# A Householder step rearranged: pairs side by side, one correction product, the p column on ScalarE, A x of block 2 on TensorE, fewer zero matmuls

## What is computed

```python
deg = jnp.sum(A, axis=0) + jnp.sum(A, axis=1) - jnp.diagonal(A)
L_norm = d_inv_sqrt[:, None] * (jnp.diag(deg) - A) * d_inv_sqrt[None, :]
_, U = jnp.linalg.eigh(L_norm)
agg = jnp.einsum('mn,bnd->bmd', U.T, features)
h = jax.nn.relu(agg @ W1 + b1)
return jnp.einsum('nm,bmd->bnd', U, h @ W2 + b2)
```

## Time and profile before

| | |
|---|---|
| three runs | 4189.59, 4192.28 and 4192.59 us, median 4192.28 us |
| span of the profiled execution | 4189.8 us |
| busy: TensorE, its loads, VectorE, ScalarE | 81%, 49%, 79%, 37% |
| x of step 2 to last x (L486) | 58.2 to 2189.7 us |

### The profile page before, as it was taken

How to read it: one execution, slowest core, us unless ns; L and a number is a source line. 1 busy time by engine, 2 the same in 40 slices (tenths; PEclk the granted TensorE clock), 3 DMA queues, 4 the chain that set the end, 5 groups by cost and what they waited for, 6 DMA issues and landing times. The chain is left out here.

```text
span 4189.8 us, 62612 instructions
## 1 busy us (share of the span) xinstructions
PE 3382.9 (81%) x14639; PEld 2049.1 (49%) x14827; DVE 3298.6 (79%) x21659; ACT 1532.1 (37%) x5534; POOL 55.6 (1%) x71
## 2 busy tenths in 40 slices
PE   5999999999999999988886576554207999998859
PEld 3555555555555665577774322243103444454337
DVE  7888898889988788999988899999984323454467
ACT  2444444333333333333332322211212324554545
POOL 0000000000000000000000000000000000020000
PEclk9999999999999899955559887755558999999969
DMA  0000000000000000000000000000002000000001
GB/s 11 1 1 1 1 1 1 1 1 1 1 1 1 1 2 2 1 1 1 1 1 1 1 1 1 1 1 1 0 20 50 0 0 0 1 0 0 0 6 36
DMA packets 14163, 16.47 MB, mean 4 GB/s; under 512 B 571, under 2 KB 10214, under 8 KB 13798
## 3 DMA queue, kind: packets, MB, share of 16 engines
q1 hardware_dynamic: 13798, 12.48, 1.1%
HBM read 8.28 MB, written 4.19 MB: 3 GB/s over the span
## 5 line engine op out<-in xcount | busy, mean ns | idle before, releaser
L206 PE MATMUL ps<-zero_stream 128*128 128x512 bf16 x2875 | 845.9, 397 | 9.0 <-issue 2.8
L206 PEld LDWEIGHTS ps<-zero_stream 128*128 128x128 bf16 x3045 | 333.6, 126 | 227.7 <-issue 101.7
L304 ACT ACTIVATE refl<-ps,tiny 128x1 f32<-128x1 f32 x511 | 133.5, 261 | 451.4 <-PE ps L244 287.9
L318 ACT ACTIVATE vectors<-WihT,refl 128x4 f32<-128x4 f32 (+2 forms) x383 | 115.0, 300 | 391.9 <-DVE refl L439 387.3
L255 PEld LDWEIGHTS ps<-dot_parts,ones 128*128 128x128 f32 x766 | 133.2, 201 | 203.6 <-DVE dot_parts L433 179.9
L233 PE MATMUL ps<-ident,vectors 128*128 128x128 f32 x1148 | 214.9, 298 | 14.3 <-DVE vectors L486 1.3
L380 DVE CUSTOM_DVE_ANT_0 products<-ps,UT 128x511 f32<-128x511 f32 (+60 forms) x426 | 215.0, 533 | 13.1 <-PE ps L233 12.5
L486 DVE SCALAR_TENSOR_TENSOR vectors<-x_scaled,ps,y_scaled 128x4 f32<-128x4 f32 (+3 forms) x510 | 116.2, 228 | 134.5 <-PE ps L255 89.9
L233 PEld LDWEIGHTS ps<-ident,vectors 128*128 128x128 f32 x1148 | 124.0, 141 | 191.6 <-DVE vectors L486 186.0
L380 DVE CUSTOM_DVE_ANT_0 products<-ps,U 128x499 f32<-128x499 f32 (+57 forms) x402 | 199.2, 524 | 5.1 <-PE ps L233 4.6
L686 ACT ACTIVATE sturm_signs<-sturm_products,sign_bias 128x576 bf16<-128x576 f32 x96 | 74.4, 775 | 350.8 <-DVE products_mark L713 350.8
(11 more groups left out here) (611 smaller groups left out, 8440.9 us busy)
## 6 DMA issues: line engine op xcount, KB each, us to landing
out_dram<-x SPq DMA_DIRECT2D x16, 256.0 KB, 2.3
adj<-in_adj_dram SPq DMA_DIRECT2D x1, 1024.0 KB, 5.2
l2w_in<-in_L_gnn_W_dram SPq DMA_DIRECT2D x2, 128.0 KB
Wqkv<-in_L_gnn_Wqkv_dram SPq DMA_DIRECT2D x1, 192.0 KB
L_gnn_W<-in_L_gnn_W_dram SPq DMA_DIRECT2D x2, 64.0 KB
L_gnn_Wg<-in_L_gnn_Wg_dram SPq DMA_DIRECT2D x2, 64.0 KB
x<-in_x_dram SPq DMA_DIRECT2D x4, 0.5 KB
L_gnn_Wo<-in_L_gnn_Wo_dram SPq DMA_DIRECT2D x1, 64.0 KB
```

Of the source, the lines that this page charges most:

```text
L206: nc.tensor.matmul(MA[t][:],still[:,0:P],still[:],start=False,stop=True,skip_group_check=True)
L304: nc.scalar.activation(s[:,u,Y:Y+1],NG[:,0:1] if wide else NG[:,1:2],ACT.Sqrt,bias=tiny[:,0:1]).then_inc(root,1)
```

## The change

- Pairs are held side by side (v, w, v, w...) instead of 32 columns apart, and the two halves of a matmul's result are swapped by reading its operand in reversed order. In blocks 0 and 1 the two correction products become one (`by_both`). The panel's transposes get a copy of the pairs made by ScalarE (`pairs_turned`), and the rows of pairs come out with two copies instead of three.
- The p column is made by ScalarE in every block, with one activation for each live tile. So is `x_below`, which VectorE made in `close`.
- `regime` cuts the steps anew: 0 is m below 128, 1 to 263, 2 to 383, 3 the rest. In regime 2 all of A x is made by TensorE (8 one-column matmuls, before 4), x is no longer transposed, and the dots are matmuls with V instead of VectorE's.
- From regime 1 on the norm has its own matmul, ahead of the pair sums.
- The table of zero matmuls has smaller numbers.
- In block 3 row m+1 is picked out by two matmuls, p's entry apart from the pairs', and the norm matmul waits for kappa in every step.
- In the last level of a later factorisation two small additions are made.

```diff
-    if b==NT-1: return (0,0,0)
-    return (1 if b<2 else 0,((6,6,9,6),(5,5,4,4),(4,4,3,5))[b][kind],2)
+    if r==3: return (0,0,0)
+    return (1 if r==0 else 0,((6,2,9,6),(4,1,4,4),(2,0,1,1))[r][kind],2)
...
+def regime(m):
+    return 0 if m<P else 1 if m<2*P+PANEL else 2 if m<3*P else 3
...
+                def row_selected(m, t):
+                    n=2+2*pending(m)[1] if pending(m) else 2
+                    early=m>=TAIL
+                    if early: nc.tensor.matmul(ROWS[:,0:1],pivot(m),XG[:,t,PC_:PC_+1],start=True,stop=True)
+                    lo=2 if early else 0
+                    nc.tensor.matmul(in_pairs(ROWS[:,lo:n]),pivot(m),swapped(XG[:,t,X_+lo:X_+n]),start=True,stop=True).then_inc(sel_ps,1)
...
+                    if r<3:
+                        if r<2:
...
+                        else: product(m,NT-1)
+                        if r: norm(m)
...
+                        if tiles: product(m,b if r==2 else NT-1)
...
+                            pe.wait_ge(y_ready,m)
+                            for t in range(b,NT):
+                                ins=nc.tensor.matmul(dots(m),V[:,t,m-1:m].broadcast_to([P,P]),XG[:,t,Y_:Y_+2],start=t==b,stop=t==NT-1)
...
-                        pe.wait_ge(e_ready,m-TAIL+1)
-                        if m==TAIL: pe.wait_ge(kap_ready,m-1)
+                        pe.wait_ge(e_ready,m-TAIL+1); pe.wait_ge(kap_ready,m-1)
...
+                    if r==2:
+                        act.wait_ge(h_ready,m)
+                        nc.scalar.activation(sh[:,sl],sub[:,sl,i],ACT.Copy,scale=s[:,u,H:H+1]).then_inc(sh_ready,1)
...
+                    act.wait_ge(y_ready,m)
+                    if r==0: act.wait_ge(s_ready,m)
+                    for t in range(b,NT):
+                        ins=nc.scalar.activation(XG[:,t,PC_:PC_+1],XG[:,t,C_:C_+1],ACT.Identity,scale=s[:,u,S_:S_+1],bias=XG[:,t,Y_:Y_+1])
+                    ins.then_inc(pc_ready,1)
...
-                        dot_parts(); inverses(); y_below(); p_column()
-                        after("ym")
-                        x_by_shift(col(Q)); y_scaled(col(Q)); x_scaled(); last="xt"
...
+                        if r==0:
+                            multiply(2); inverse(); sign(); multiply(3)
+                            by_both(); reflector(); corrections(); denominator()
+                            column_of_A(); matrix_times_x(); inverses(); dot_parts()
+                        elif r==1:
+                            multiply(1); inverse(); multiply(3); sign(); twice_norm(); by_both(); shift(); corrections()
+                            reflector(); column_of_A(); matrix_times_x(); denominator(); dot_parts(); inverses()
+                        else:
+                            by_rows(); sign(); inverse(); by_dots(); twice_norm(); corrections(); reflector(); shift()
+                            column_of_A(); denominator(); matrix_times_x(); inverses()
```

292 lines of the change are left out of this document (149 added, 143 removed).

## The result

The changed kernel takes 4677.9 us (median; 4667.6 to 4691.9), the kernel before 4190.9 beside it: a ratio of 1.119, 95% interval 1.114 to 1.124. The forecast was 4520 us, in a range from 4270 to 4800. The profiled execution has a span of 4675.8 us, 486.0 above the one of before.

What follows compares the result with a forecast made beforehand. No engine is always busy, so the order of one step was taken to bound the kernel. 4190 + 75 (block 0) + 35 (block 1) + 54 (block 3) + 166 (block 2) = 4520 us, range 4270 to 4800.

Steps and rivals of the forecast that it cites:

- The p column on ScalarE: Blocks 0 to 2: activations at 0.29 us each lengthen the chain to a step's first instruction, +0.67, +0.40, +0.12 us a step.
- Block 2 at half clock: Block 2: clock falls early and stays low, steps of 5.2 us, +166 us instead of 14; likeliest case, chance 0.38.
- Block 3: Block 3: the second row matmul's two passes add 0.43 us to each of 127 steps, +54 us; kappa's wait over by then.
- the clock in blocks 0 and 1: Blocks 0 and 1: fewer zero matmuls may lose the clock more often; taken as nothing, with 0 to 300 us as ends.
- the third case: Blocks 0 and 1 fall to half clock too: block 1 +165 us, 4685 us in all, up to 4850; chance 0.17.
- The merged product: Block 0: saves some 0.07 us, but the reduction waits for ScalarE; taken as even, 0.1 us a step either way.
- the fourth case: Faster: activations pass in 0.09 us each and the clock holds, 4172 us; deciding point 0.13 us an activation; chance 0.12.

Runs made afterwards that it cites:

- e6: The kernel before with the p column made by ScalarE, one activation for each live tile, in all blocks: 4346.7 us, ratio 1.041.
- e1: The changed kernel with the p column back on VectorE in blocks 0 to 2: 4539.8 us, ratio to before 1.087.
- e2: The changed kernel with the table of zero matmuls of before: 4697.9 us.
- e4: The changed kernel with p column on VectorE in blocks 0 to 2, old zero table and one row matmul in block 3: 4474.1 us, ratio 1.070.
- e5: The kernel before with the change's shorter table of zero matmuls alone: 4347.6 us, ratio 1.042.
- e3: The changed kernel with the row picked out by one matmul in block 3, the wait for kappa kept: 4641.2 us.
- e8: The changed kernel with p column, zero table, A x of block 2 and single row matmul as before, kappa waited for once: 4218.7 us.
- e9: e8 without the one zero matmul behind the row's matmul in block 1 (m 128 to 255): 4262.5 us.
- e10: e8 with more zero matmuls in the first step of each panel, and one more at panel ends in blocks 1 and 2: 4181.8 us.
- e11: e10 with two correction products in block 2, as before the change, and one long multiply left out in first steps of panels: 4167.5 us.

## Why the prediction was right, and where its sum was off

The direction and the range were right, and each mechanism that it named is there. The forecast was 158 us short.

- **The p column on ScalarE**: four L348 at 0.28 us (forecast 0.29), y to L380 1.87 us (1.93), L380 released by ScalarE. For the column +75 us were forecast in block 0 and, before the gains of other parts, (0.40 + 0.04) x 136 = 60 in block 1. Alone it costs 94 and 46 (e6), and its removal gives 93 and 37 (e1). The chain was right, and a little too long. What was not in it are the falls of the clock that longer steps bring in block 0 (0.95 to 0.89 in e6), and the update step at half clock, where the sum had the tile copy end 0.27 us behind y and it ends 2.1 us behind it.
- **Block 2 at half clock**: forecast 5.2 us a step and +166, measured 5.17 in plain steps and +170.6. The choice rested on the reading that busy time alone doesn't keep the clock, and e2 and e4 show it (99.9% busy at 0.55 and 0.59). The reason given, fewer long matmuls, is enough by itself (e5), but so is A x on TensorE with the zero matmuls of before (e4), which the forecast had only as work at half clock. So the +170.6 divides by the order in which one counts: 82 for the table first (e5) and 88 for the rest (629.5 - 541.0), or 248 for the rest first (e2, 706.8 - 458.9) and 77 given back by the shorter table.
- **Block 3**: forecast +54, measured +54.7, and yet the step behind it failed. I put all of it on the two passes of L230 and called the wait for kappa over by then. That held only as long as L230 stood ahead of it. Taken away, the matmul gives 0.26 us a step (e3) and the wait another 0.16 (e8). A wait that ends just before another one hides behind it, and a right sum says nothing of how it divides: here it came out by luck. (The wait alone, with L230 in place, wasn't taken away.)
- **The term that was mis-sized is the clock in blocks 0 and 1**: taken at nothing, with 0 to 300 us as the ends. The sum missed 48 us in block 0 (122.5 - 75) and 101 in block 1 (135.9 - 35), and the runs put them there. This was the third case, held at 0.17, and its time was 4685, 7 us from the measured; its half-clock step of block 1, worked out as 5.9 us, is 5.81. Its time fits in part by luck: it has all of block 1 at half clock and block 0 untouched, where block 1 was at 0.64 and block 0 at 0.76. The argument "dips cost before as well, and cost less with fewer zero matmuls in the queue" weighed the price of a fall and not how many there are: 87 steps of block 1 over 5 us for 11. I had the row that speaks against it, block 3 at 0.50 without zero matmuls, and used it for block 2 alone.
- **What wasn't priced at all**: the zero matmul behind the row in block 1, which goes by `r==0` for `b<2`. It stood in the quoted diff. e9 prices it at 38 us. With the table (40) and the column (46) alone, and the 53 of e4, block 1 adds up to 139 of 136, though nothing says that such costs must add up; block 0 (17 + 94 - 6 = 105 of 122.5) leaves 17 us. The update step above shows what can make it: at half clock the tile copy comes late, and the p column behind it. That share was not tried by itself.
- **The merged product**: taken as even in block 0, with 0.1 us a step either way. With the p column and the table taken back, plain steps of block 0 at full clock are 0.09 us longer than before (4.85 for 4.76, e4), so it and the new order lose a little; the first steps of a panel win 0.4. In block 1 it and the norm's own matmul were to give 0.18 us a step, and do: 3.94 for 4.12 in plain steps at full clock (e8, e10). In block 2 the old two products are the better ones (e11).
- **Two slips that change nothing**: the stretch of block 0 in the earlier trace rows has 126 steps, 5.40 us each, not 127 of 5.36; and the point at which the fourth case decides is 0.12 us an activation, not 0.13, if the gain of block 1 is held at the 0.18 that the case allows.

## What to carry to other kernels

Where TensorE's clock decides, count the long matmuls that each kind of step gives it, one by one, before and after: removing one filler of 0.22 us can cost more than its own length (here 38 us over 128 steps, 0.30 each), though nobody waits for it. A low busy share of an engine is no room to move work to; look how long before its due time the last result of the old order was there. And undo each part both ways, in the new kernel and alone in the old one, since a wait can hide behind another and either of two parts can be enough to lose the clock.
